# Differential attention over 32 chunks: a loop of four lanes against a pipeline of one chunk a slot, with block-wise scores

## The chip, the cores and the metric

The kernel runs on one core of a Trainium2 chip. The metric is the device time of one execution in microseconds (us). A core has five engines that run side by side and meet at semaphores: TensorE (PE in the profile, its weight loads PEld), VectorE (DVE), ScalarE (ACT), GpSimd (POOL) and SyncE (SP), which here only issues DMAs.

## The reference

Six layers follow one another, each added to its input after a LayerNorm without weights: cross-attention, differential attention, a gated feed-forward layer, an adapter attention, a second attention and a layer of eight experts. Only the second, differential attention, is touched. Its core, cut to what matters:

```python
b, t, e = x.shape                                   # 128 sequences, 32 tokens, 256 features
q = (x @ wq.T).reshape(b, t, NH2, HALF)             # NH2 = 4 half-heads of HALF = 64
k = (x @ wk.T).reshape(b, t, NH2, HALF)
v = (x @ wv.T).reshape(b, t, H, 2 * HALF)           # H = 2 heads of 128
q = _apply_rope(q, cos, sin)
k = _apply_rope(k, cos, sin)
scores = jnp.einsum('bhtd,bhsd->bhts', q, k) / SCALING      # SCALING = 128 ** -0.5
probs = jax.nn.softmax(scores, axis=-1)
lam = lam1 - lam2 + LAMBDA_INIT
probs = probs.reshape(b, H, 2, t, t)
diff = probs[:, :, 0] - lam * probs[:, :, 1]
attn = jnp.einsum('bhts,bhsd->bhtd', diff, v)
attn = attn * jax.lax.rsqrt(jnp.mean(attn * attn, axis=-1, keepdims=True) + EPS)
attn = attn * subln_weight
return attn.transpose(0, 2, 1, 3).reshape(b, t, e) @ wout.T
```

The softmax runs over the 32 tokens of a sequence for each of four half-heads; the probabilities of two half-heads are subtracted with a factor lambda, and the result weighs v. Then comes an RMS norm for each head and the output projection. All is in float32.

## The kernel before, in words

The 128 x 32 tokens are 4096 rows, cut into 32 chunks of 128 rows. So one chunk holds four whole sequences of 32 tokens, one under the other on the partitions. Each of the six layers is a phase of its own with a barrier behind it (`phase`, L2600), so the engines start every phase together.

`differential_attention` (L1294) works on four chunks a turn, one in each of its LANES, in eight turns: seven in a hardware loop (`turns`, L1355) and the last written out behind it. Every engine goes through one step for all four lanes before the next step. The front part of a turn (LayerNorm, transpose, the projections to q, k and v, the rotation) is done for the next turn ("ahead") in the middle of the present one. Tiles exist once for each lane. In PSUM, `TurnRing` (L1206) hands the eight banks round: each step of each lane takes the next bank, and PE waits until what the bank held before has been moved out.

The steps for one chunk are these. VectorE computes bn_stats, bn_aggr and var_eps; GpSimd raises to the power -0.5 (inv_std, L1406); VectorE writes xn (L1590). PE transposes xn (L1432), ScalarE copies it to SBUF (xn_t, L1507), PE projects q and k into one bank of 512 columns (L1445) and v into 256. VectorE multiplies by the cosines (turn_cos, L1598, 512 wide) and, swapped in pairs, by the sines (L1599, L1600, 256 wide each), straight from PSUM, and adds (qk, L1603). PE turns qk over (four transposes); ScalarE copies q_t (L1515) and two half-filled copies of k (k_own, L1518), in which the rows of the other half-head are zero. PE multiplies full 128x128 arrays (L1458): each chunk's 128 queries against all its 128 keys, for four half-heads, so three quarters of the scores are between different sequences. VectorE scales them and adds the mask `same` (-1e30 between sequences, L1611), 128x512 in all, and reduces the negative maximum (L1616). ScalarE takes the exponential with a row sum for each half-head (L1525), each followed by a read of the accumulator. VectorE forms reciprocal, lambda factor, the weighed second half and diff (L1621 to L1626); PE transposes diff, ScalarE copies it, PE multiplies by v (av, L1471). ScalarE squares and sums (L1531), VectorE forms ms (L1632), GpSimd inv_rms (L1413), VectorE attn with both factors (L1637). PE transposes attn, ScalarE copies it, PE applies w_o (L1482), VectorE adds the residual x_res, which was loaded a second time, and SyncE stores y.

Semaphores count by lane and turn; on every engine the order is that of the source.

Of the kernel before, what the change touches and what calls it, by code (L numbers as in the profile page):

```python
# [1205 lines left out]
class TurnRing:  # L1206

    def __init__(self, items, turns, ahead=(), banks=8):
        assert len(items) % banks == 0, len(items)
        self.items, self.banks, self.turns, self.ahead = items, banks, turns, ahead
        self.per_bank = len(items) // banks
        self.of_stage = {s: [n for t, n in items if t == s] for s, _ in items}

    def bank(self, stage, n):  # L1220
        return self.items.index((stage, n)) % self.banks

    def _earlier(self, stage, n, keep):

        at = self.items.index((stage, n))
        return [self.items[k] for k in range(at % self.banks, at, self.banks) if keep(self.items[k][0])]

    def full(self, t, stage, n):

        is_ahead = lambda s: s in self.ahead  # L1230
        if isinstance(t, int) and t == 0 and stage in self.ahead:
            return 1 + len(self._earlier(stage, n, is_ahead))
        first = len([1 for s, k in self.items if s in self.ahead and self.bank(s, k) == self.bank(stage, n)])
        if isinstance(t, int) and t == self.turns - 1 and stage not in self.ahead:
            return first + t * self.per_bank + 1 + len(self._earlier(stage, n, lambda s: not is_ahead(s)))
        body = self.per_bank if stage in self.ahead else 0
        return t * self.per_bank + (first + 1 + len(self._earlier(stage, n, lambda s: True)) - body)

    def out(self, t, stage, n, back=0):

        own = self.of_stage[stage]
        return t * len(own) + (own.index(n) + 1 + len(own) * (1 - back))

    def before(self, t, stage, n):

        is_ahead = lambda s: s in self.ahead
        if isinstance(t, int) and t == 0 and stage in self.ahead:
            held = self._earlier(stage, n, is_ahead)
            return (held[-1][0], self.out(0, *held[-1])) if held else None
        last = isinstance(t, int) and t == self.turns - 1 and stage not in self.ahead  # L1250
        held, wrap = self._earlier(stage, n, (lambda s: not is_ahead(s)) if last else (lambda s: True)), 0
        if not held:
            held, wrap = [(s, k) for s, k in self.items if self.bank(s, k) == self.bank(stage, n)], 1
        s, k = held[-1]
        back = wrap + (stage in self.ahead) - (s in self.ahead)
        return s, self.out(t, s, k, back=back)


# [1383 lines left out]
```

## Time and profile before

| what | us |
|---|---|
| median of three runs | 3857.2 |
| lowest and highest | 3856.8, 3860.03 |
| the profiled execution | 3863.55 |
| its span, first to last instruction | 3861.8 |
| the stage of differential attention, first load to last residual add | 996.71 to 1307.38 |
| one turn of its loop (four chunks) | 35.3 |

Over the span PE is busy 91%, VectorE 66%, ScalarE 52% and GpSimd 39%, at a mean granted clock of TensorE of 0.961 of full speed. These are averages over six phases; for a change to one phase the windows and the timeline of this phase count.

How to read the rows further down. A row of the timeline has the start, the time, the engine, the line, the operation, what is written and read, the shape and the number of instructions, and in brackets the idle time ahead and what ended it; a row for several instructions runs from the first start to the last end. A row of the windows has the stretch, its length, for PE, PEld, DVE, ACT and POOL the busy time with the number of instructions, the granted clock of TensorE, the share of DMA time and GB/s. A row of the groups has after the bar the busy time in all and the mean in ns, then the idle time ahead of the group. A row of the waits has who waited for whom, us in total, how often, and the longest. A row of one line's instructions gives ns as minimum, median and maximum. A float32 product appears as two matmuls, a transpose as one.

### The profile page before, as it was taken

To read this page: it belongs to the slowest core of one execution; us is meant where nothing else is said; L and a number is where in the kernel's file an instruction comes from. 1 tells how busy PE (TensorE), PEld (TensorE's weight loads), DVE (VectorE), ACT (ScalarE), POOL (GpSimd) and SP (SyncE) were. 2 spreads that over 40 slices of the span, in tenths; PEclk is the share of its full clock that TensorE was granted. 3 is DMA by queue.
4 is the path that set the end of the run, shared out by engine and by line. 5 is a ranking of instruction groups with operands and counts; after the bars stand their busy time and mean duration, and the time that the engine had idled before them with its cause. 6 is when DMAs were issued, how large, how long until landed. Compare 5 with 4: busy or idle time off the path is not lost. (4 is left out here: it accounts for less than half of the span.)

```text
span 3861.8 us, 99724 instructions
## 1 busy us (share of the span) xinstructions
PE 3515.5 (91%) x32616; PEld 2584.1 (67%) x32616; DVE 2541.8 (66%) x7637; ACT 1991.8 (52%) x6079; POOL 1509.7 (39%) x3070
## 2 busy tenths in 40 slices
PE   7999999999477797999999999999968869999999
PEld 5777777777355575777777777777746545555555
DVE  4667777777577554888888888888845543344333
ACT  4777777777255444666666666676632211111111
POOL 3566666666111253555555555555520000000000
PEclk9999999999789898999999999999978969999999
DMA  3111111111111123111111111111145650000000
GB/s 82 54 52 50 51 52 52 52 52 40 49 49 49 51 82 93 42 44 43 41 45 42 41 47 40 41 47 40 37 94 128 131 146 18 16 16 16 16 16 16
DMA packets 355951, 200.53 MB, mean 52 GB/s; under 512 B 186126, under 2 KB 350822, under 8 KB 355830
## 3 DMA queue, kind: packets, MB, share of 16 engines
q1 hardware_dynamic: 335669, 189.95, 17.7%
q10 hardware_dynamic: 20160, 8.92, 1.2%
q8 instruction: 82, 1.34, 0.2%
q14 instruction: 40, 0.32, 0.0%
HBM read 154.12 MB, written 40.40 MB: 50 GB/s over the span
## 5 line engine op out<-in xcount | busy, mean ns | idle before, releaser
L1004 ACT ACTIVATE probs_a<-s_ps_a,neg_max_a 128x257 f32<-128x257 f32 x1024 | 474.0, 474 | 368.6 <-DVE neg_max_a L1101 368.6
L1047 POOL TENSOR_SCALAR probs_a<-probs_a,gated_a 128x256 f32<-128x256 f32 x1024 | 497.4, 504 | 310.9 <-DVE gated_a L1109 310.9
L1101 DVE TENSOR_REDUCE neg_max_a<-s_ps_a 128x1 f32<-128x257 f32 x1024 | 361.2, 415 | 0.0
L2458 ACT ACTIVATE gate_e<-bank_e 128x512 f32<-128x512 f32 x128 | 76.4, 597 | 493.4 <-PE bank_e L2431 493.3
L498 POOL TENSOR_SCALAR probs_i<-probs_i,inv_sum_i 128x256 f32<-128x256 f32 x512 | 256.9, 515 | 136.9 <-DVE inv_sum_i L631 135.6
L2390 POOL TENSOR_TENSOR inv_std_e<-var_eps_e,half_e 128x1 f32<-128x1 f32 x32 | 16.5, 541 | 654.0 <-DVE var_eps_e L2489 654.0
L2572 DVE TENSOR_TENSOR hidden_e<-gate_e,bank_e 128x512 f32<-128x512 f32 x128 | 87.4, 688 | 276.1 <-PE bank_e L2431 274.3
L476 ACT ACTIVATE probs_i<-s_ps_i,neg_max_i 128x257 f32<-128x257 f32 x512 | 235.9, 473 | 49.8 <-DVE neg_max_i L692 48.7
L862 PE MATMUL c_ps_a<-ctx_t_a,w_qk_a 128*128 128x256 f32 x1024 | 256.9, 394 | 0.0
L908 PE MATMUL a_ps_a<-w_v_a,ctx_t_a 128*128 128x256 f32 x1024 | 255.3, 392 | 0.0
L369 PE MATMUL a_ps_i<-w_k_i,ctx_t_i 128*128 128x256 f32 x1024 | 253.1, 390 | 1.4 <-issue 0.2
L385 PE MATMUL c_ps_i<-w_v_i,ctx_t_i 128*128 128x256 f32 x1024 | 243.4, 381 | 0.0
L2431 PE MATMUL bank_e<-xn_t_e,w_gate_e 128*128 128x512 f32 x512 | 242.8, 597 | 0.0
L2431 PE MATMUL bank_e<-xn_t_e,w_up_e 128*128 128x512 f32 x512 | 240.6, 592 | 0.0
L692 DVE TENSOR_REDUCE neg_max_i<-s_ps_i 128x1 f32<-128x257 f32 x512 | 182.0, 418 | 80.8 <-PE s_ps_i L427 80.8
L862 PEld LDWEIGHTS c_ps_a<-ctx_t_a,w_qk_a 128*128 128x128 f32 x1024 | 185.2, 191 | 69.3 <-issue 36.0
L908 PEld LDWEIGHTS a_ps_a<-w_v_a,ctx_t_a 128*128 128x128 f32 x1024 | 184.1, 190 | 69.2 <-issue 49.5
L2409 PE MATMUL bank_e<-w_down_e,hidden_e 128*128 128x256 f32 x1024 | 230.2, 379 | 0.0
L2409 PEld LDWEIGHTS bank_e<-w_down_e,hidden_e 128*128 128x128 f32 x1024 | 194.7, 190 | 50.2 <-issue 26.8
L1004 ACT ACTIVATION_READ_ACCUMULATOR probs_a<-s_ps_a,neg_max_a 128x1 f32 x1024 | 207.5, 203 | 0.0
L369 PEld LDWEIGHTS a_ps_i<-w_k_i,ctx_t_i 128*128 128x128 f32 x1024 | 185.3, 191 | 32.7 <-issue 6.3
L869 PE MATMUL s_ps_a<-k_t_a,q_bd_a 32*128 32x289 f32 x2048 | 197.1, 454 | 2.3 <-DVE k_t_a L1188 1.8
(352 smaller groups left out, 8171.5 us busy)
## 6 DMA issues: line engine op xcount, KB each, us to landing
ctx_t_i<-in_ctx_t SPq DMA_DIRECT2D x128, 256.0 KB, 2.7
ctx_t_a<-in_ctx_t SPq DMA_DIRECT2D x128, 256.0 KB, 2.7
mask_a<-in_L_xattn_mask SPq DMA_DIRECT2D x512, 4.0 KB, 1.5
v_bd_a<-v_self_a SPq DMA_DIRECT2D x512, 8.0 KB, 1.8
x_tok_i<-in_x SPq DMA_DIRECT2D x32, 128.0 KB, 2.0
x_res_i<-in_x SPq DMA_DIRECT2D x32, 128.0 KB, 2.5
x_after<-y_tok_i SPq DMA_DIRECT2D x32, 128.0 KB, 1.8
x_tok_d<-x_after SPq DMA_DIRECT2D x32, 128.0 KB, 2.1
```

The source lines that it names most:

```text
L369: last = pe.matmul(a_ps[:, r * D:r * D + D], ctx_t[at.b(2)][:, c, r * P:r * P + P], w_k[:, c, :], start=c == 0, stop=c == 1)
L385: last = pe.matmul(c_ps[:, r * D:r * D + D], ctx_t[at.b(1)][:, c, r * P:r * P + P], w_v[:, c, :], start=c == 0, stop=c == 1)
L476: act.activation(probs[:, i, :], s_ps[i][:, 0:K], ACT.Exp, bias=neg_max[:, i:i + 1], accum_out=row_sum[:, i:i + 1]).then_inc(exp_done, 1)
L498: pool.tensor_scalar(probs[:, i, 0:2 * P], probs[:, i, 0:2 * P], inv_sum[:, i:i + 1], 1.0, ALU.mult, ALU.mult).then_inc(probs_ready, 1)
L862: last = pe.matmul(into[:, f * n:f * n + n], w_qk[:, c, D + f * P:D + f * P + P], ctx[:, c, 0:n], start=c == 0, stop=c == 1)
L869: pe.matmul(s_ps[:, g, 0:N], q_bd[j][rows, f, :, :].rearrange("p h q -> p (h q)"), k_t[j][rows, f, :], start=True, stop=True).then_inc(sco ...
L908: last = pe.matmul(a_ps[:, r * D:r * D + D], ctx_t[at.b(1)][:, c, r * P:r * P + P], w_v[:, c, :], start=c == 0, stop=c == 1)
L1004: act.activation(probs[:, t, :], s_ps[:, g, 0:K], ACT.Exp, bias=neg_max[:, t:t + 1], accum_out=row_sum[:, t:t + 1]).then_inc(exp_done, 1)
L1047: pool.tensor_scalar(probs[:, t, 0:2 * P], probs[:, t, 0:2 * P], gated[:, t:t + 1], 1.0, ALU.mult, ALU.mult).then_inc(probs_ready, 1)
L1101: dve.tensor_reduce(neg_max[:, 4 * f + g:4 * f + g + 1], s_ps[:, g, 0:K], AX.X, ALU.max, negate=True).then_inc(max_ready, 1)
L2409: last = pe.matmul(w[:, t * D:t * D + D], hidden[e % 2][:, k, tok:tok + P], w_down[:, e, k, :], start=k == 0, stop=k == TILES - 1)
L2431: last = pe.matmul(w[:, :], weights[:, e, c, t * P:t * P + P], xn_t[:, c, :], start=c == 0, stop=c == 1)
```

## The change

The function is rewritten; `TurnRing`, the mask and the loop are gone.

- One chunk enters each slot, and the slots, from -3 to 34, are written out one after another without a loop. In slot n the statistics and xn are those of chunk n+3, the transpose of xn is that of n+2, projections and rotation those of n+1, scores to diff those of n, av, squares and inv_rms those of n-1, the scaling, the output projection and the store those of n-2.
- Most tiles exist once. v has three copies, diff_t and y two, x_tok eight; the residual is taken from x_tok, so the second load goes. PSUM has fixed places: a bank each for qk, the transposed qk, av, the transposed attn and y, one shared by v and the transposed xn, and two for the scores.
- Scores are formed for each sequence by itself: 4 sequences x 2 half-heads x 2 heads, products of 64 rows by 32 columns each, side by side in tiles of the array. The result is 128x128 a chunk, 32 keys a half-head, and needs no mask. av is formed in the same manner, 32 rows by 32 columns by 128.
- VectorE reduces the maximum and subtracts it (top, centred); one exponential of 128 columns takes the place of four, with the scale in it and without a row sum, which is a reduction on VectorE.
- diff is turned over by VectorE in blocks of 32x32 (transpose to diff_t) in place of PE and a copy.
- The projection of q and k is copied to SBUF by ScalarE (qk_raw); the two sine products and xn move from VectorE to GpSimd. Scaling attn by inv_rms moves to ScalarE; the weight subln is multiplied into w_o once.
- The loads at the start are split over SyncE's and ScalarE's queue with a semaphore each.

```diff
-    stages = ["qkT", "s0", "s1", "xT", "qk", "dT", "av", "v", "aT", "out"]
-    ring = TurnRing([(s, a) for s in stages for a in range(LANES)], CHUNKS // LANES, ahead=FRONT)
+        SLOTS = range(-3, CHUNKS + 3)
...
+                if live(n + 1):
+                    pairs, sines = (x.rearrange("p (f two) -> p f two", two=2) for x in (qk_raw[:, :], rope[:, 1, :]))
+                    dst = turn_sin[:, :].rearrange("p (f two) -> p f two", two=2)
+                    pool.wait_ge(qk_read, n + 2)
+                    pool.tensor_tensor(dst[:, :, 0], pairs[:, :, 1], sines[:, :, 0], ALU.mult)
+                    pool.tensor_tensor(dst[:, :, 1], pairs[:, :, 0], sines[:, :, 1], ALU.mult).then_inc(sin_ready, 1)
...
+                if live(n - 1):
+                    pool.wait_ge(ms_ready, n)
+                    pool.tensor_tensor(inv_rms[:, :], ms[:, :], half[:, :], ALU.pow).then_inc(rms_ready, 1)
...
+                    pe.wait_ge(qk_t_ready, n + 1)
+                    ge(pe, centred_ready, n)
+                    for c in range(2):
+                        for s in range(4):
+                            own = slice(L * s, L * s + L)
+                            for r in range(2):
+                                rows = slice(HALF * r, HALF * r + HALF)
+                                last = pe.matmul(s_ps[own, r, c * L:c * L + L], qk_t[rows, c, own], qk_t[rows, 2 + c, own], start=True, stop=True)
...
+                if live(n - 2):
+                    act.wait_ge(rms_ready, n - 1)
+                    for h in range(2):
+                        last = act.activation(attn[:, h, :], av_ps[:, h * P:h * P + P], ACT.Copy, scale=inv_rms[:, h:h + 1])
+                    last.then_inc(attn_ready, 1)
+                if live(n + 1):
+                    act.wait_ge(qk_full, n + 2)
+                    ge(act, qk_ready, n + 1)
+                    act.activation(qk_raw[:, :], qk_ps[:, :], ACT.Copy).then_inc(qk_read, 1)
...
+                    dve.wait_ge(exp_done, n + 1)
+                    after(dve.tensor_reduce(row_sum[:, :], probs[:, :, :], AX.X, ALU.add))
+                    after(dve.reciprocal(inv_sum[:, :], row_sum[:, :]))
+                    after(dve.tensor_scalar(inv_sum[:, 2:4], inv_sum[:, 2:4], neg_lam[:, :], None, ALU.mult))
+                    after(dve.tensor_tensor(weighed[:, :, :], probs[:, :, :], inv_sum[:, :].unsqueeze(2).broadcast_to([P, 4, L]), ALU.mult))
+                    after(dve.tensor_tensor(diff[:, :].rearrange("p (c k) -> p c k", c=2), weighed[:, 0:2, :], weighed[:, 2:4, :], ALU.add))
+                    ge(dve, av_full, 4 * (n - 1))
+                    dve.transpose(diff_t[n % 2][:, :], diff[:, :]).then_inc(diff_ready, 1)
+                if live(n - 1):
+                    dve.wait_ge(ss_ready, n)
+                    dve.tensor_scalar(ms[:, :], ss[:, :], 1.0 / P, 1e-5, ALU.mult, ALU.add).then_inc(ms_ready, 1)
```

`after` makes VectorE wait for the instruction before; `ge` waits only where the count is over zero. The function `statistics`, called between the add qk and row_sum, holds bn_stats, bn_aggr and var_eps.

PE's order first. Before, in the last turn (the loop's body has the front steps of the next turn between the scores and the diff transposes), each row is a step of four lanes:

```order
L1432 MATMUL bank_d<-const_d,qk_d 128x128 x16
L1458 MATMUL bank_d<-k_own_d,q_t_d 128x128 x16
L1432 MATMUL bank_d<-const_d,diff_d 128x128 x8
L1471 MATMUL bank_d<-v_d,diff_t_d 128x128 x8
L1432 MATMUL bank_d<-const_d,attn_d 128x128 x8
L1482 MATMUL bank_d<-w_o_d,attn_t_d 128x256 x8
```

Now, one slot from the middle, each row a step of one chunk:

```order
L1348 MATMUL qk_ps_d<-w_qk_d,xn_t_d 128x512 x2
L1354 MATMUL qk_t_ps_d<-ident_d,qk_d 128x128 x4
L1361 MATMUL vx_ps_d<-w_v_d,xn_t_d 128x256 x2
L1371 MATMUL s_ps_d<-qk_t_d 32x32 x16
L1378 MATMUL vx_ps_d<-ident_d,xn_d 128x128 x2
L1384 MATMUL at_ps_d<-ident_d,attn_d 128x128 x2
L1393 MATMUL av_ps_d<-v_d,diff_t_d 32x128 x8
L1402 MATMUL y_ps_d<-w_o_d,attn_t_d 128x256 x2
```

The transposes of diff are gone from PE, the scores stand behind the projection of the next chunk's v, and all eight steps of a slot are of different chunks.

VectorE's order. Before, a part of the last turn, from the last mask to the first lane's diff:

```order
L1611 SCALAR_TENSOR_TENSOR masked_d<-bank_d,same_d 128x256
L1616 TENSOR_REDUCE neg_max_d<-masked_d 128x4
L1621 RECIPROCAL inv_sum_d<-row_sum_d 128x4
L1622 TENSOR_SCALAR inv_sum_d<-inv_sum_d,neg_lam_d 128x2
L1623 TENSOR_TENSOR masked_d<-probs_d,inv_sum_d 128x256
L1626 SCALAR_TENSOR_TENSOR diff_d<-probs_d,inv_sum_d,masked_d 128x128 x2
```

Now, in a middle slot, from the maximum to the block transpose; ahead of it stands turn_cos, behind it ms and y:

```order
L1481 TENSOR_REDUCE top_d<-s_ps_d 128x4
L1482 TENSOR_TENSOR centred_d<-s_ps_d,top_d 128x128
L1488 TENSOR_TENSOR qk_d<-turn_cos_d,turn_sin_d 128x512
L1459 BN_STATS stats_d<-x_tok_d 128x6
L1461 BN_AGGR mean_var_d<-stats_d 128x2
L1462 TENSOR_SCALAR var_eps_d<-mean_var_d 128x1
L1496 TENSOR_REDUCE row_sum_d<-probs_d 128x4
L1497 RECIPROCAL inv_sum_d<-row_sum_d 128x4
L1498 TENSOR_SCALAR inv_sum_d<-inv_sum_d,neg_lam_d 128x2
L1499 TENSOR_TENSOR weighed_d<-probs_d,inv_sum_d 128x128
L1500 TENSOR_TENSOR diff_d<-weighed_d 128x64
L1502 STREAM_TRANSPOSE diff_t_d<-diff_d 128x64
```

Between the maximum and the row sum of one chunk there now stand the add for the next chunk and the statistics of the chunk three on.

GpSimd's order. Before, in the loop's body (two rows of four for each kind shown):

```order
L1406 TENSOR_TENSOR inv_std_d<-var_eps_d,half_d 128x1
L1412 ISA
L1413 TENSOR_TENSOR inv_rms_d<-ms_d,half_d 128x2
L1412 REGISTER_ALU
L1413 TENSOR_TENSOR inv_rms_d<-ms_d,half_d 128x2
```

Now, one slot:

```order
L1326 TENSOR_TENSOR turn_sin_d<-qk_raw_d,rope_d 128x256
L1327 TENSOR_TENSOR turn_sin_d<-qk_raw_d,rope_d 128x256
L1330 TENSOR_TENSOR inv_std_d<-var_eps_d,half_d 128x1
L1333 TENSOR_SCALAR xn_d<-x_tok_d,mean_var_d,inv_std_d 128x256
L1336 TENSOR_TENSOR inv_rms_d<-ms_d,half_d 128x2
```

inv_rms now stands behind the sine products and xn of later chunks.

## Rows read from the trace of the kernel before

**Rows 1.** Timeline at the stage's edges, and from the DMA issues the load of rope (last number: us to landing).

```profile
996.71 1.78 SPq L1370 DMA_DIRECT2D x_tok_d<-x_after  x4
...
1306.96 0.42 DVE L1643 TENSOR_TENSOR y_d<-bank_d,x_res_d 128x256 f32<-128x256 f32 x1 [0.44 <-PE bank_d L1482]
...
rope_d<-in_L_attn_rope SPq DMA_DIRECT2D x1, 512.0 KB, 3.6
```

**Rows 2.** Windows, one turn of the loop.

```profile
1098.30:1133.60 35.30, 27.05 (x136) 19.31 (x135) 26.65 (x80) 18.55 (x76) 4.82 (x8) 0.90 0.14 45
```

**Rows 3.** Waits in the seven turns, 1027.5 to 1275.5.

```profile
PE bank_d L1432 <- DVE xn_d L1590: 43.1, 7, 6.2
...
DVE masked_d L1611 <- PE bank_d L1458: 27.5, 28, 3.0
```

**Rows 4.** ScalarE: a group of 128-wide squares, and two 512-wide copies in the timeline.

```profile
L1531 ACT ACTIVATE squares_d<-bank_d 128x128 f32<-128x128 f32 x64 | 17.1, 273 | 1.9 <-PE bank_d L1471 1.2
...
1325.21 1.08 ACT L1844 ACTIVATE xs_g<-bank_g 128x512 fp32r<-128x512 f32 x2 [0.50 <-PE bank_g L1779]
```

**Rows 5.** PE's timeline in three other stages: transposes, tiles, a projection.

```profile
703.89 0.60 PE L414 MATMUL a_ps_i<-const_i,probs_i 128*128 128x128 f32 x4
...
704.86 0.69 PE L427 MATMUL s_ps_i<-k_n_i,q_bd_i 32*64 32x257 f32 x16
706.17 0.65 PE L437 MATMUL out_ps_i<-probs_t_i,v_i 128*32 128x64 f32 x32 [0.62 <-ACT probs_t_i L472]
...
2685.48 1.88 PE L920 MATMUL b_ps_a<-w_qk_a,xn_t_a 128*128 128x512 f32 x4
...
2905.23 2.48 PE L2112 MATMUL s_ps_r<-by_dim_k_r,by_dim_q_r 32*32 32x64 f32 x128 [0.29 <-DVE attn_r L2296]
```

**Rows 6.** What ended the idle time ahead of L427's weight loads.

```profile
  issue: 22.6, 128
```

**Rows 7.** VectorE: groups by form, and four adds in the timeline.

```profile
L1550 DVE TENSOR_TENSOR lam_in_d<-lam_in_d 128x128 f32<-128x128 f32 x1 | 0.3, 293 | 9.7 <-DMA lam_in_d<-in_L_attn_lambda_k 9.7
...
1125.54 2.48 DVE L1603 TENSOR_TENSOR qk_d<-turn_cos_d,turn_sin_d 128x512 f32<-128x512 f32 x4
...
L1578 DVE BATCH_NORM_STATS2 stats_d<-x_tok_d 128x6 f32<-128x256 f32 x32 | 11.2, 412 | 0.0
...
L1621 DVE RECIPROCAL inv_sum_d<-row_sum_d 128x4 f32<-128x4 f32 x32 | 5.5, 171 | 0.0
...
L1622 DVE TENSOR_SCALAR inv_sum_d<-inv_sum_d,neg_lam_d 128x2 f32<-128x2 f32 x32 | 7.3, 229 | 1.1
...
L1623 DVE TENSOR_TENSOR masked_d<-probs_d,inv_sum_d 128x256 f32<-128x256 f32 x32 | 13.6, 426 | 1.1
...
L685 DVE STREAM_TRANSPOSE p_last_t_i<-p_last_i 128x32 f32<-128x32 f32 x32 | 6.5, 204 | 0.9 <-POOL p_last_i L494 0.9
```

**Rows 8.** Timeline of one turn: from ms over inv_rms to attn.

```profile
1128.18 1.37 POOL L1413 TENSOR_TENSOR inv_rms_d<-ms_d,half_d 128x2 f32<-128x2 f32 x2 [13.90 <-DVE ms_d L1632]
...
1129.00 0.35 DVE L1637 SCALAR_TENSOR_TENSOR attn_d<-bank_d,inv_rms_d,subln_d 128x128 f32<-128x128 f32 x1 [0.70 <-POOL inv_rms_d L1413]
```

**Rows 9.** GpSimd's groups of 256 columns in two other stages.

```profile
L498 POOL TENSOR_SCALAR probs_i<-probs_i,inv_sum_i 128x256 f32<-128x256 f32 x512 | 256.9, 515 | 136.9 <-DVE inv_sum_i L631 135.6
...
L1060 POOL TENSOR_TENSOR self_p_a<-self_e_a,self_inv_a 128x256 f32<-128x256 f32 x128 | 78.6, 614 | 0.0
...
L505 POOL TENSOR_TENSOR v_last_i<-v_last_raw_i,const_i 128x256 f32<-128x256 f32 x32 | 27.3, 853 | 0.0
```

**Rows 10.** One VectorE line of the first stage.

```profile
L674 DVE TENSOR_SCALAR xn_i<-x_tok_i,mean_var_i,inv_std_i x32: 414/931/933, 24.5 to 925.1; 128x256 f32<-128x256 f32 x32
```

**Rows 11.** PE's timeline behind its long idle time, and a window inside it.

```profile
1113.23 2.24 PE L1432 MATMUL bank_d<-const_d,xn_d 128*128 128x128 f32 x8 [6.16 <-DVE xn_d L1590]
...
1110.30:1111.30 1.00, 0.00 (x0) 0.00 (x0) 1.00 (x4) 0.00 (x0) 0.00 (x0) 0.50 0.00 0
```

More of the change, by code:

```diff
@@ L1203, in _ @@
             every_slot(dve, FIRST, TURNS, slot)
[L1206 to L1256, printed above, removed]
 LANES = 4
@@ L1351, in moved @@
-        def moved(i, stage, a, back=0):
-            return out_of[stage], ring.out(i, stage, a, back=back)
-        def turns(eng, body):
-            with eng.Fori(0, TURNS - 1) as i:
-                body(i, i + 1)
-            body(TURNS - 1, None)
-        def free_banks(eng, name):
-            for s in stages:
-                if mover[s] == name:
-                    eng.sem_inc(out_of[s], LANES)
+        x_tok = [sb(f"x_tok{j}", [P, D]) for j in range(X_TILES)]
+        stats, mean_var, var_eps, inv_std = sb("stats", [P, 6]), sb("mean_var", [P, 2]), sb("var_eps", [P, 1]), sb("inv_std", [P, 1])
@@ new lines, in differential_attention @@
+        xn, xn_t = sb("xn", [P, D]), sb("xn_t", [P, 2, P])
+        qk_raw, turn_cos, turn_sin, qk = (sb(n, [P, 2 * D]) for n in ("qk_raw", "turn_cos", "turn_sin", "qk"))
+        qk_t = sb("qk_t", [P, 4, P])
+        v = [sb(f"v{j}", [P, D]) for j in range(3)]
+        top, centred, probs = sb("top", [P, 4]), sb("centred", [P, 4, L]), sb("probs", [P, 4, L])
+        row_sum, inv_sum = sb("row_sum", [P, 4]), sb("inv_sum", [P, 4])
+        weighed, diff = sb("weighed", [P, 4, L]), sb("diff", [P, 2 * L])
@@ L1365, in differential_attention, with live @@
+        at_full, at_ready, y_full, y_ready = sem("at_full"), sem("at_ready"), sem("y_full"), sem("y_ready")
+        step = sem("step")
+        SLOTS = range(-3, CHUNKS + 3)
         block = stack.enter_context(nc.Block())
+        def live(n):
+            return 0 <= n < CHUNKS
         @block.sync
         def _(sp):
[L1369 to L1379 removed]
@@ L1403, in front @@
-            def front(t):
-                for a in range(LANES):
-                    pool.wait_ge(ln_dve, n_of(t, a))
-                    pool.tensor_tensor(inv_std[a][:, :], var_eps[a][:, :], half[:, 0:1], ALU.pow).then_inc(ln_pool, 1)
-            def body(i, ahead):
-                if ahead is not None:
-                    front(ahead)
-                for a in range(LANES):
-                    pool.wait_ge(ms_ready, n_of(i, a))
-                    pool.tensor_tensor(inv_rms[a][:, :], ms[a][:, :], half[:, :], ALU.pow).then_inc(inv_rms_ready, 1)
@@ L1418, in _ @@
         @block.tensor
         def _(pe):
-            pe.wait_ge(loaded, 16 * 12)
-            def item(i, stage, a):
-                held = ring.before(i, stage, a)
-                if held:
-                    pe.wait_ge(out_of[held[0]], held[1])
-                n = ring.bank(stage, a)
-                return bank[n], full[n]
-            def turn_over(i, stage, a, src, count):
-                w, f = item(i, stage, a)
-                for c in range(count):
-                    last = pe.transpose(w[:, c * P:c * P + P], src(c), ident)
-                last.then_inc(f, 1)
```

425 lines of the change are left out of this document (174 added, 251 removed).

## Prediction, made before the changed kernel was run

> **What bounds the kernel now.** I read the windows of the stage first, then its waits, then the timeline. The change touches one stage of six, so only that stage's time can move: it runs from the first load at 996.71 to the last residual add, which ends at 1307.38 (1306.96 + 0.42), 310.7 us of the 3861.8 us span [rows 1]. Inside, a turn of the loop takes 35.3 us for four chunks, 8.8 us a chunk, and no engine fills it: PE 27.1, VectorE 26.7, ScalarE 18.6, GpSimd 4.8 us [rows 2]. The waits say why: the four lanes go through each step together, so the engines take turns. PE waits for xn once a turn, 43.1 us in seven turns, up to 6.2 at once, and VectorE for the scores, 27.5 us [rows 3]. The bound is the hand-over between engines in a turn, not an engine. A pipeline with one chunk a slot attacks just that, and the question is what the slot's own longest loop is.
>
> **The slot, step by step.** In the new order GpSimd's inv_rms for chunk n-1 comes last in slot n; ScalarE's first step of the next slot (scaling attn) waits for it, and everything behind it on ScalarE queues, the copies qk_raw and qk_t among them. The scores wait for qk_t, VectorE's maximum for the scores, and VectorE then runs in order down to ms, for which inv_rms waits. That is a closed loop, and its length is the slot. From mark to mark (the start of the attn scaling):
> - attn, two copies of 128 from PSUM, 0.27 each alone, overlapped to the next start: 0.35; qk_raw, 512 wide, two of which take 1.08, so 0.60 alone and 0.48 to the next start: 0.50; qk_t, whose end counts: 0.60 + 0.04 hop [rows 4]. Together 1.49.
> - scores: 16 products are 32 matmuls here, in tiles of 64 rows x 32 columns. No such tile is in the trace. From below, 32 matmuls of 64 columns in 128x32 tiles take 0.65 and 16 of 257 columns in 32x64 tiles 0.69. From above, 128 strided ones in 32x32 tiles take 2.48, 0.62 for 32; tiles of 64 rows number half as many, and if only half as many run side by side it is 1.24 [rows 5]. The first row is nearest in instructions and width (even a little wider), so I take 0.70 + 0.04.
> - top and centred, each over 128 columns, 0.29 alone: 0.29 + 0.04, and 0.25 to the next start [rows 7]. Together 0.58.
> - the add qk, 512 wide: four in 2.48, the last 0.68, so 0.60 to 0.62 [rows 7].
> - statistics of chunk n+3: 0.41, then two short ones that wait for each other, 0.34 with the gaps (0.16 and less each, by the shortest rows here): 0.75 [rows 7].
> - row_sum 0.29, reciprocal 0.17, the factor 0.23, weighed (128) 0.29, diff (64) 0.22, the block transpose of 64 columns 0.24 (0.20 for 32), and five gaps of 0.035 (1.1 us over 32): 1.64 [rows 7].
> - ms 0.16 and a hop of 0.08; inv_rms, two of which take 1.37, 0.70 and a hop of 0.10 (in the timeline 0.12, from 1128.18 + 0.70 to 1129.00): 1.04 [rows 8].
> The sum is 1.49 + 0.74 + 0.58 + 0.62 + 0.75 + 1.64 + 1.04 = 6.86 us.
>
> **What GpSimd's new work adds.** It takes over the two sine products (256 wide, strided) and xn. A product of that width is 0.61 where nothing hinders it and 0.85 in the first stage [rows 9]. The sines start 1.03 after the mark and the add wants them at 2.81: two at 0.61 end at 2.25, two at 0.85 at 2.73, and if they first wait out turn_cos (0.68) they end at 2.93, which pushes the add by 0.16. Then pow (below the 0.70 of inv_rms) and xn (0.50) on GpSimd lie beside VectorE's weighed and diff. A VectorE instruction can be held for the whole of a GpSimd one: xn_i has a median of 931 ns and a minimum of 414, and the difference is just GpSimd's 515 [rows 9, 10]. So 0 to 0.5 there. I take 0.15 and 0.25, in all 0.4: both meetings happen in every slot, but neither is sure to overlap in full. The slot is 7.25 us, with 6.8 and 7.6 for nothing and everything of this, and 0.5 more if the scores are at their upper end. The Trainium skill (GPSIMD Engine Reference, section Engine selection) says not to put two-input elementwise work on GpSimd, as it is about 2x slower there than on VectorE; this case's rows say 0.61 against 0.43 for VectorE's 256-wide product [rows 7, 9], 1.4x; by twice 0.43 the sines would be 1.72 together, end at 2.75, and still make the add. The rule would be right about the work but not about the loop, because VectorE is in the loop and GpSimd between 1.0 and 2.8 is not.
>
> **The other engines in a slot.** PE: 1.72 + 0.86 + 0.86 for the projections (four instructions of 512 columns in 1.88, so 0.43 each, and half for 256), 0.44 + 0.22 + 0.22 for transposes (four in 0.60, some 0.16 of it latency), 0.60 for scores, 0.45 for av: 5.4 us [rows 5]. It changes its tiling four times a slot. The weight loads of the tiled group at L427 stand idle 22.6 us over 128 groups, 0.18 each; four times that makes 6.1 us [rows 6]. ScalarE 3.6 us, GpSimd 3.1. All are under 7.25, so the other work that goes (masking of 128x128, four exponentials with a read each for one, half-empty k copies) pays only as far as it shortens the loop.
>
> **From slot to stage.** 31 slots separate the marks of slots 1 and 32: 31 x 7.25 = 224.8, less 2.9 as slots 29 to 31 lack statistics and the last the add. Ahead: the loads, where rope (3.6 us to land) [rows 1] holds GpSimd's start to about 1001.5; LayerNorm, a transpose, the projection, rotation, the second transpose and its copy, one after another and partly at the lower clock, 9.5 us to where slot 0's mark would be at 1010 or so; slot 0 with the lambda arithmetic (a 512-wide product and four small ones, 1.6), but without inv_rms, 7 to 9: mark 1 at about 1018.7, 22 us after the first load. Behind mark 32: scaling, av, squares, inv_rms, scaling, transpose, copy, output product 1.03, add 0.42: 6.3. Sum 22 + 221.9 + 6.3 = 250.2 against 310.7: 60.5 us gone. The profiled execution took 3863.55; so 3803; it lies 6.35 over the median of the three runs, which moves alike, to 3797. Outside the stage nothing changes.
>
> **Rivals.**
> - **The loop is longer** (8.1, from 7.75 to 8.8): scores at 1.24, GpSimd holding VectorE for full instructions twice a slot, hops of two waits each. For it: strided operands on GpSimd aren't in the trace, and loops added up leave out small gaps. Against: each piece's row is at hand. 7.25 + 0.85 gives 31 x 0.85 = 26 more: 3823.
> - **The loop is shorter** (6.7): nothing meets on GpSimd, and start-up takes 20: 3797 - 17 - 2 = 3778.
> - **Slower: PE at its lower clock.** In the loop of before PE stands idle for 6.16 us a turn up to 1113.23, and in the microsecond from 1110.30 the granted clock is 0.50, 1.2 GHz [rows 11]. The new slot leaves PE idle in one piece of 1.2 to 2 us, each slot. If the clock goes down there, PE's 5.4 us double to about 10.4 and PE becomes the bound: 31 x 3.15 = 98, 3895 in all. It decides from a slot of 9.2 us on, that is with some 60% of the slots at 1.2 GHz. For it: the idle piece comes every slot. Against: in the loop of before it takes the long idle piece to bring it down, and a PE that has become the bound has no idle left to lower it. No row shows what a piece of 1 to 2 us does.
> - **It does not do what it says:** the straight-line code of 38 slots (the loop of before was one body) or single buffers make slots wait so that 8.85 a chunk stays; 3850 to 3865. Per slot PE needs some 150 instructions in 7 us. Nothing in the trace shows a wait for code of that size.
>
> **Numbers.** Forecast 60%, longer loop 22%, shorter 8%, no change 4%, slower 6%. The likeliest gives 3797. The range takes the longer loop in: a slot of 8.35 gives 31 x 1.1 = 34, so 3832 above; the shorter loop gives 3776 below. A measurement of this kernel can tell about 0.2%, 8 us, from no change; the forecast and both loops lie beyond. Faster 0.90, same 0.04, slower 0.06.
>
> **What would show it.** Right: ScalarE's attn scalings 7.25 us apart (6.9 to 7.7), ahead of each a wait for inv_rms; VectorE waiting for the scores about 1 us a slot and for qk_raw; clock 1.00 from slot 2 on; the last add about 250 us after the first load; VectorE busy some 4.8 us a slot. Wrong step by step: an idle time ahead of the add qk that ends with the sines (GpSimd too slow); weighed or diff over 0.4 us (held port); scores over 1 us; 0.50 in the clock rows inside the stage; PE without idle time at all. A stage at 250 us and a kernel that didn't move would mean another stage gave it back.

## The result and the profile after

The changed kernel takes 3800.3 us (median of four runs, 3797.7 to 3809.5) against 3857.2 us (3856.8 to 3860.0): a ratio of 0.9856 with an interval of 0.984 to 0.9872, 57 us less. The forecast was 3797, with a range of 3776 to 3832, and the measured time lies inside. The profiled execution took 3809.5 us, its span is 3807.7 us, 54.1 less than before. But the stage gave only part of it. Its edges, from the timeline, and the load of rope from the DMA issues:

```profile
998.04 0.36 SPq L1300 DMA_DIRECT2D x_tok_d<-x_after  x1
...
1263.95 0.42 DVE L1509 TENSOR_TENSOR y_d<-y_ps_d,x_tok_d 128x256 f32<-128x256 f32 x1 [3.26 <-PE y_ps_d L1402]
...
1267.59 0.33 SPq L1572 DMA_DIRECT2D ident_g<-in_const  x1
...
rope_d<-in_L_attn_rope ACTq DMA_DIRECT2D x1, 512.0 KB, 6.1
```

From the first load to the last add it is 266.3 us where it was 310.7 [rows 1]: 44.4 us gone, not the 60.5 of the forecast. With the gap to the next stage's first DMA it is 269.6 against 313.9. The remaining 10 us of the two profiles' 54.1 came mostly from a stage that the change does not touch; more on that below. The other 3 us of the 57 come from the choice of execution: the profiled one lies 9.2 us above its median here, 6.4 before.

The slot. Starts of ScalarE's attn are 7.62 or 7.63 us apart in 27 slots of the 31; two windows of a slot each (columns as in [rows 2]):

```profile
1114.74:1122.36 7.62, 7.06 (x77) 4.57 (x75) 4.62 (x15) 3.35 (x13) 4.75 (x5) 1.00 0.12 37
1122.36:1129.98 7.62, 5.96 (x63) 3.89 (x64) 4.62 (x15) 3.46 (x12) 4.75 (x5) 0.78 0.12 34
```

GpSimd is busy 4.75 us, not the 3.1 forecast. The granted clock is 1.00 in one slot and 0.78 in the other, and both last 7.62: TensorE's clock does not set the slot. It is 0.78 in eight of the 27 equal slots. In the last steps, with nothing else in flight, the clock does count. These are the window from the last attn to the end of the last add, and in it the last output product, first in this profile and then in that of e12, which differs only by a table that is loaded and not used:

```profile
1260.00:1264.37 4.37, 2.98 (x7) 1.46 (x6) 0.85 (x2) 1.01 (x3) 0.00 (x0) 0.50 0.09 30
...
1261.84 2.07 PE L1402 MATMUL y_ps_d<-w_o_d,attn_t_d 128*128 128x256 f32 x4 [0.47 <-ACT attn_t_d L1437]
...
1253.59:1256.77 3.18, 1.57 (x6) 0.88 (x6) 0.42 (x1) 1.01 (x3) 0.00 (x0) 1.00 0.12 41
...
1255.18 1.13 PE L1409 MATMUL y_ps_d<-w_o_d,attn_t_d 128*128 128x256 f32 x4 [0.47 <-ACT attn_t_d L1445]
```

At a clock of 0.50 it takes 4.37 us, at 1.00 3.18. The start differs as well: the first attn comes 32.8 us after the first load here and 30.9 in e12, whose stage is 4.7 us shorter with the same slot. So one profile tells the stage to some 5 us, and the slot much better.

The waits of the loop, 1025 to 1235, where [rows 3] had PE waiting for xn and VectorE for the scores:

```profile
ACT attn_d L1417 <- POOL inv_rms_d L1336: 95.9, 27, 3.6
...
DVE turn_cos_d L1478 <- ACT qk_raw_d L1422: 49.0, 27, 2.1
...
DVE qk_d L1488 <- POOL turn_sin_d L1327: 14.8, 27, 0.6
DVE top_d L1481 <- PE s_ps_d L1371: 10.1, 27, 0.4
```

And the chain of one slot, from its timeline:

```profile
1122.36 0.62 ACT L1417 ACTIVATE attn_d<-av_ps_d,inv_rms_d 128x128 f32<-128x128 f32 x2 [3.64 <-POOL inv_rms_d L1336]
1122.87 0.60 ACT L1422 ACTIVATE qk_raw_d<-qk_ps_d 128x512 f32<-128x512 f32 x1
...
1123.50 0.69 DVE L1478 TENSOR_TENSOR turn_cos_d<-qk_raw_d,rope_d 128x512 f32<-128x512 f32 x1 [1.81 <-ACT qk_raw_d L1422]
1123.55 1.35 POOL L1326 TENSOR_TENSOR turn_sin_d<-qk_raw_d,rope_d 128x256 f32<-128x256 f32 x1 [1.22 <-ACT qk_raw_d L1422]
...
1124.01 0.36 PE L1371 MATMUL s_ps_d<-qk_t_d 64*32 64x32 f32 x32 [1.95 <-ACT qk_t_d L1425]
...
1124.86 0.84 POOL L1327 TENSOR_TENSOR turn_sin_d<-qk_raw_d,rope_d 128x256 f32<-128x256 f32 x1
1124.89 0.29 DVE L1482 TENSOR_TENSOR centred_d<-s_ps_d,top_d 128x128 f32<-128x128 f32 x1
...
1125.73 0.69 DVE L1488 TENSOR_TENSOR qk_d<-turn_cos_d,turn_sin_d 128x512 f32<-128x512 f32 x1 [0.55 <-POOL turn_sin_d L1327]
...
1127.04 0.20 ACT L1444 ACTIVATION_READ_ACCUMULATOR squares_d<-av_ps_d 128x1 f32 x1
...
1127.89 1.37 POOL L1333 TENSOR_SCALAR xn_d<-x_tok_d,mean_var_d,inv_std_d 128x256 f32<-128x256 f32 x1
...
1128.20 0.46 DVE L1500 TENSOR_TENSOR diff_d<-weighed_d 128x64 f32<-128x64 f32 x1
...
1128.86 0.13 DVE L1505 TENSOR_SCALAR ms_d<-ss_d 128x2 f32<-128x2 f32 x1
...
1129.23 0.72 POOL L1336 TENSOR_TENSOR inv_rms_d<-ms_d,half_d 128x2 f32<-128x2 f32 x1
```

The loop is the one forecast, except for one stretch. The scores' way was open at 1125.18, when centred ended; the add qk began at 1125.73, when the second sine product had ended. So the loop runs over the sines: 1.19 us from attn to the first sine product, 2.18 for both and the hop, 0.61 for the add to its next start, 0.74 statistics, 1.78 from row_sum to ms, 0.37 to inv_rms, 0.75 to the next attn: 7.62. All of it is in a fixed order on each engine, so a step waits for what stands before it even where its input is there: the squares were done at 1127.24, while inv_rms began at 1129.23.

### The profile page after: what moved, and what is told of

Read it like the earlier page. It is cut to its first block and busy times, and to the rows that moved or that the text cites. A ratio compares the mean times of both kernels' runs of the same rounds, so it can differ in the third digit from the quotient of the medians.

```text
span 3807.7 us, 100837 instructions
## 1 busy us (share of the span) xinstructions
PE 3493.5 (92%) x33704; PEld 2547.5 (67%) x33704; DVE 2475.0 (65%) x7474; ACT 1951.9 (51%) x5855; POOL 1621.9 (43%) x3166
## 5 line engine op out<-in xcount | busy, mean ns | idle before, releaser
L363 PEld LDWEIGHTS a_ps_i<-w_k_i,ctx_t_i 128*128 128x128 f32 x1024 | 185.6, 191 | 32.8 <-issue 6.4
```

The lines of the kernel that those rows point to most:

```text
L363: last = pe.matmul(a_ps[:, r * D:r * D + D], ctx_t[at.b(2)][:, c, r * P:r * P + P], w_k[:, c, :], start=c == 0, stop=c == 1)
```

## Experiments

Theory A: the slot is the closed loop over inv_rms, lengthened by GpSimd. Theory B: PE with its tilings is the bound. Theory C: VectorE's work is. "Stage" below is first DMA to first DMA of the next stage in the profile, "rest" the span less the stage, "slot" the usual spacing of attn's starts in the middle of the stage (before: a turn over four). Stage, slot and rest are of one profiled execution each. The variants e1 to e8, e11 and e12 are of the changed kernel, e9 and e10 of the one before. e11 leaves out the swap of pairs and the mean, and is a single run. Ratios are against the kernel before on the same chip.

| kernel | median us | ratio (interval) | stage | slot | rest |
|---|---|---|---|---|---|
| before | 3857.2 | | 313.9 | 8.83 | 3547.9 |
| after | 3800.3 | 0.9856 (0.984-0.9872) | 269.6 | 7.62 | 3538.1 |
| e1, ms early | 3762.4 | 0.9751 (0.9733-0.977) | 224.9 | 6.24 | 3536.7 |
| e2, xn on VectorE | 3792.7 | 0.9827 (0.9807-0.9846) | 255.9 | 7.21 | 3535.6 |
| e3, output product twice | 3800.7 | 0.9854 (0.9836-0.9872) | 266.6 | 7.63 | 3528.6 |
| e4, cosines from PSUM | 3791.2 | 0.9822 (0.9802-0.9842) | 254.6 | 7.12 | 3539.0 |
| e5, ms first | 3748.5 | 0.9706 (0.969-0.9723) | 213.2 | 5.87 | 3535.6 |
| e6, e1 and e4 | 3764.7 | 0.9754 (0.9738-0.977) | 232.0 | 6.42 | 3530.7 |
| e7, scores twice | 3799.9 | 0.9846 (0.9829-0.9862) | 269.5 | 7.63 | 3529.4 |
| e8, sines on VectorE | 3786.0 | 0.981 (0.9794-0.9827) | 253.7 | 7.20 | 3533.0 |
| e9, before again | 3856.6 | 1.0001 (0.9992-1.0011) | 315.9 | | 3541.6 |
| e10, before written out | 3852.1 | 0.9992 (0.9982-1.0001) | 315.6 | | 3532.0 |
| e11, plain GpSimd | 3776.0, one run | | 244.9 | 6.83 | 3529.3 |
| e12, mask table kept | 3794.9 | 0.9846 (0.9829-0.9862) | 264.9 | 7.62 | 3527.8 |

**e1: ms and inv_rms earlier.** In both engines' order only:

```diff
                     after(dve.reciprocal(inv_sum[:, :], row_sum[:, :]))
+                    if live(n - 1):
+                        dve.wait_ge(ss_ready, n)
+                        dve.tensor_scalar(ms[:, :], ss[:, :], 1.0 / P, 1e-5, ALU.mult, ALU.add).then_inc(ms_ready, 1)
...
                     pool.tensor_tensor(inv_std[:, :], var_eps[:, :], half[:, 0:1], ALU.pow).then_inc(ln_pool, 1)
+                if live(n - 1):
+                    pool.wait_ge(ms_ready, n)
+                    pool.tensor_tensor(inv_rms[:, :], ms[:, :], half[:, :], ALU.pow).then_inc(rms_ready, 1)
+                if live(n + 3):
                     pool.wait_ge(ln_pool, n + 4)
```

> The same work in another order: ms of chunk n-1 stands behind the reciprocal on VectorE and no longer behind the block transpose, and inv_rms stands ahead of xn on GpSimd. Theory A (the slot is the closed loop that inv_rms ends): in the changed kernel's middle slot the squares were done at 1127.24 but inv_rms began only at 1129.23; here it can begin at about 1127.9, so 1.3 us less a slot, a slot of 6.1 to 6.4 until PE's own 5.4 to 6.1 us is next: 31 x 1.2 = 37, some 3762 us. Theory B (PE with its tiling switches is the bound): nothing moves, 3795 to 3803. Theory C (VectorE's sum of work and short gaps is the bound, about 7 us a slot): 10 us or less.

Measured: 3762.4 us, slot 6.24. The same instructions, and 1.38 us a slot less. Timeline:

```profile
1125.88 0.17 DVE L1501 TENSOR_SCALAR ms_d<-ss_d 128x2 f32<-128x2 f32 x1
...
1126.13 0.70 POOL L1333 TENSOR_TENSOR inv_rms_d<-ms_d,half_d 128x2 f32<-128x2 f32 x1
...
1126.82 1.23 POOL L1337 TENSOR_SCALAR xn_d<-x_tok_d,mean_var_d,inv_std_d 128x256 f32<-128x256 f32 x1
...
1126.86 0.63 ACT L1418 ACTIVATE attn_d<-av_ps_d,inv_rms_d 128x128 f32<-128x128 f32 x2 [2.25 <-POOL inv_rms_d L1333]
```

The mark (the start of attn) follows inv_rms at once, as before the edit. The 1.38 us are the time from row_sum to ms, 0.52 instead of 1.78, and from ms to inv_rms, 0.25 instead of 0.37. That shows theory A and rules out B and C: on both engines the instructions are the same.

**e2: xn back on VectorE**, behind y:

```diff
-                    pool.tensor_scalar(xn[:, :], x_tok[(n + 3) % X_TILES][:, :], mean_var[:, 0:1], inv_std[:, :], ALU.subtract, ALU.mult).then_inc(xn_ready, 1)
...
+                    dve.tensor_scalar(xn[:, :], x_tok[(n + 3) % X_TILES][:, :], mean_var[:, 0:1], inv_std[:, :], ALU.subtract, ALU.mult).then_inc(xn_ready, 1)
```

> One part undone: xn goes back to VectorE, at the end of its slot, where it waits for qk_raw anyway. Theory A: inv_rms no longer stands behind xn (0.2 to 0.3 us) and diff is not stretched (0.45 to 0.22), VectorE's 0.41 more lies in its idle time: 0.4 to 0.5 us less a slot, 3785 us. Theory B: nothing. Theory C: 0.41 more a slot, 3813 us. If GpSimd's instruction holds VectorE's, diff will be 0.22 to 0.25 here; if diff is slow by itself it stays at 0.45.

```profile
1126.97 0.22 DVE L1497 TENSOR_TENSOR diff_d<-weighed_d 128x64 f32<-128x64 f32 x1
...
1127.40 0.13 DVE L1502 TENSOR_SCALAR ms_d<-ss_d 128x2 f32<-128x2 f32 x1
...
1127.61 0.70 POOL L1333 TENSOR_TENSOR inv_rms_d<-ms_d,half_d 128x2 f32<-128x2 f32 x1 [1.03 <-DVE ms_d L1502]
```

The slot is 0.41 shorter, as expected: diff takes 0.22 without xn beside it (0.46 with it), and from ms to inv_rms it is 0.21 instead of 0.37. VectorE's additional 0.41 cost nothing. The stage fell by 14 us, but the kernel's time by 8, less than the 15 expected, and the intervals of this and the changed kernel just touch; it is the slot that shows it.

**e3: the output product twice.**

```diff
-                    for c in range(2):
+                    for c in range(4):
```

(with `c % 2` in the operands)

> The output product is formed twice (four more matmuls of 256 columns a slot, 0.8 to 0.9 us of PE), at the end of PE's slot. Theory A: PE has 1.5 to 2 us of idle time there, so nothing or up to 3 us in all: 3798 to 3803. Theory B (PE is the bound): 0.85 x 31 = 26 us more, 3826.

```profile
1130.81 1.99 PE L1402 MATMUL y_ps_d<-w_o_d,attn_t_d 128*128 128x256 f32 x8
```

Eight matmuls take 1.99, four 1.13 at full clock (e12's row above): 0.86 us more of PE in each slot, and the slot is 7.63. B is out a second time.

**e7: the scores twice**, the 32 matmuls repeated:

```diff
-                    for c in range(2):
+                    for t in range(4):
+                        c = t % 2
...
```

> The 32 matmuls of the scores are run twice a slot. They lie in the loop, unlike the output product of e3. One set takes 0.36 us in the trace. Theory A: the slot grows by 0.33 to 0.36, 31 x 0.34 = 10.5 us, 3811, though only 0.34 us of PE are added where 0.86 off the loop cost nothing. Theory B: nothing to 3 us.

```profile
1130.91 0.76 PE L1372 MATMUL s_ps_d<-qk_t_d 64*32 64x32 f32 x64 [1.61 <-ACT qk_t_d L1426]
...
1131.74 0.29 DVE L1482 TENSOR_REDUCE top_d<-s_ps_d 128x4 f32<-128x128 f32 x1 [0.64 <-PE s_ps_d L1372]
...
1132.64 0.69 DVE L1489 TENSOR_TENSOR qk_d<-turn_cos_d,turn_sin_d 128x512 f32<-128x512 f32 x1 [0.29 <-POOL turn_sin_d L1327]
```

A miss: 3799.9 and a slot of 7.63, no change. top comes 0.27 later (2.48 after the mark, not 2.21), and the wait ahead of the add shrinks from 0.55 to 0.29. So the scores are not on the path; the sines are, with half a microsecond to spare beside them. I had counted the scores into the loop although the trace already showed the add waiting for the sines.

**e4: turn_cos from PSUM**, ahead of the copy:

```diff
-                    dve.wait_ge(qk_read, n + 2)
-                    dve.tensor_tensor(turn_cos[:, :], qk_raw[:, :], rope[:, 0, :], ALU.mult).then_inc(cos_ready, 1)
+                    dve.wait_ge(qk_full, n + 2)
+                    dve.tensor_tensor(turn_cos[:, :], qk_ps[:, :], rope[:, 0, :], ALU.mult).then_inc(cos_ready, 1)
...
+                    act.wait_ge(cos_ready, n + 2)
                     act.activation(qk_raw[:, :], qk_ps[:, :], ACT.Copy).then_inc(qk_read, 1)
```

> turn_cos reads the projection straight from PSUM, ahead of ScalarE's copy qk_raw, which waits for it; VectorE is idle there. So no VectorE product over two SBUF operands runs beside the first sine product. If VectorE's product holds GpSimd's (0.69 of the 1.35 us), the first sine product falls to 0.66 to 0.85, the add qk starts 0.5 us earlier, behind centred, and the slot is 0.5 us shorter: 3785 us. If the strides make it slow, it stays at 1.3 us and the time stays at 3800, or rises a few us as qk_raw comes later.

```profile
1143.60 0.68 DVE L1479 TENSOR_TENSOR turn_cos_d<-qk_ps_d,rope_d 128x512 f32<-128x512 f32 x1
...
1144.35 0.62 ACT L1417 ACTIVATE attn_d<-av_ps_d,inv_rms_d 128x128 f32<-128x128 f32 x2 [3.13 <-POOL inv_rms_d L1336]
...
1145.54 0.84 POOL L1326 TENSOR_TENSOR turn_sin_d<-qk_raw_d,rope_d 128x256 f32<-128x256 f32 x1 [1.22 <-ACT qk_raw_d L1423]
...
1146.33 0.85 POOL L1327 TENSOR_TENSOR turn_sin_d<-qk_raw_d,rope_d 128x256 f32<-128x256 f32 x1
...
1146.88 0.29 DVE L1483 TENSOR_TENSOR centred_d<-s_ps_d,top_d 128x128 f32<-128x128 f32 x1
...
1147.22 0.69 DVE L1489 TENSOR_TENSOR qk_d<-turn_cos_d,turn_sin_d 128x512 f32<-128x512 f32 x1
```

The first sine product fell from 1.35 to 0.84: the turn_cos beside it had added 0.51. The add now begins 2.87 after the mark instead of 3.37, and the slot fell by 0.50. The stage fell by 15 us and the kernel's time by 9, of 15 expected; its interval just touches that of the changed kernel. The edit does two things at once: turn_cos reads PSUM, and it is over before the sines begin. No run separates them. But in the changed kernel the second sine product runs beside top and centred, which read PSUM, and takes 0.84, so that VectorE's work alone does not hold GpSimd. The Trainium skill (SBUF — State Buffer, section "SBUF: two separate sides") describes a port pair shared by the two engines, taken as a lock by a VectorE instruction with two SBUF inputs or by GpSimd. The first sine product agrees nearly: turn_cos had 0.64 us to go when it began, and it took 0.51 longer. The same page of the Trainium skill also says that the loser waits for the whole instruction; diff does not agree: it grew by 0.24 us beside an xn of 1.37 and ended 0.60 before it.

**e8: the sines on VectorE**, behind turn_cos:

```diff
-                    pool.tensor_tensor(dst[:, :, 0], pairs[:, :, 1], sines[:, :, 0], ALU.mult)
-                    pool.tensor_tensor(dst[:, :, 1], pairs[:, :, 0], sines[:, :, 1], ALU.mult).then_inc(sin_ready, 1)
...
+                    dve.tensor_tensor(dst[:, :, 0], pairs[:, :, 1], sines[:, :, 0], ALU.mult)
+                    dve.tensor_tensor(dst[:, :, 1], pairs[:, :, 0], sines[:, :, 1], ALU.mult).then_inc(sin_ready, 1)
```

> One part undone: the two sine products are back on VectorE, behind turn_cos, reading qk_raw. By the trace: turn_cos to 1124.19, two products at 0.43 to 1125.05, top and centred to 1125.68, add from 1125.72, where it began at 1125.73 with GpSimd. So by this the slot changes by 0 to 0.25 us, and pow and xn are not earlier, 3798 to 3806: the work that was moved away was hidden, but only as far as it then held up the add. If the products over strided SBUF operands are slower than 0.43 on VectorE (0.6), 0.3 to 0.4 more a slot, 3812.

```profile
1128.71 0.42 DVE L1475 TENSOR_TENSOR turn_sin_d<-qk_raw_d,rope_d 128x256 f32<-128x256 f32 x1
...
1129.05 0.42 DVE L1476 TENSOR_TENSOR turn_sin_d<-qk_raw_d,rope_d 128x256 f32<-128x256 f32 x1
...
1129.91 0.68 DVE L1486 TENSOR_TENSOR qk_d<-turn_cos_d,turn_sin_d 128x512 f32<-128x512 f32 x1
```

A miss to the good side: 3786.0, slot 7.20. I had counted 0.43 for each sine product on VectorE; they take 0.42, but the next instruction starts 0.34 after each, and the add begins 2.95 us after the mark (1126.96) instead of 3.37. Moving the sines to GpSimd cost 0.42 us a slot. Its interval (0.9794 to 0.9827) lies wholly below that of the changed kernel.

**e11: what makes GpSimd slow.** e4 with plain operands:

```diff
-                    pool.tensor_tensor(dst[:, :, 0], pairs[:, :, 1], sines[:, :, 0], ALU.mult)
+                    pool.tensor_tensor(turn_sin[:, 0:D], qk_raw[:, 0:D], rope[:, 1, 0:D], ALU.mult)
...
-                    pool.tensor_scalar(xn[:, :], x_tok[(n + 3) % X_TILES][:, :], mean_var[:, 0:1], inv_std[:, :], ALU.subtract, ALU.mult).then_inc(xn_ready, 1)
+                    pool.tensor_scalar(xn[:, :], x_tok[(n + 3) % X_TILES][:, :], inv_std[:, :], None, ALU.mult).then_inc(xn_ready, 1)
```

> As e4 (turn_cos from PSUM, so that nothing holds GpSimd), but the sine products read and write plain 256-column halves instead of every second column, and xn is one operation, a product with inv_std, instead of a subtraction and a product; the pair swap and the mean are left out, only the durations count. If the stride makes 0.84 us out of 0.61, the sine products take 0.61 here; if GpSimd takes that long for any product of 256 columns in this stage, 0.84. If the second operation makes xn 1.37, it takes 0.5 to 0.75 here; if it is contention with VectorE's products, 1.2 or more.

The groups, 1025 to 1200:

```profile
L1333 POOL TENSOR_SCALAR xn_d<-x_tok_d,inv_std_d 128x256 f32<-128x256 f32 x26 | 27.9, 1074 | 2.6
...
L1327 POOL TENSOR_TENSOR turn_sin_d<-qk_raw_d,rope_d 128x256 f32<-128x256 f32 x25 | 18.2, 728 | 0.0
```

Between the two guesses: the stride makes 0.12 of the 0.84 us, the second operation (or the second scalar that it reads) 0.30 of the 1.37. Another 0.14 goes with what runs beside it: in e1, where xn stands behind weighed and diff and not beside them, it takes 1.23. Why a product with a scalar takes 1.07 here and 0.515 in the first stage [rows 9] stays open.

**e5 and e6: how far it goes.** e5 places ms right behind the add qk, ahead of the statistics, and inv_rms right behind the sines, ahead of pow:

```diff
+                if live(n - 1):
+                    dve.wait_ge(ss_ready, n)
+                    dve.tensor_scalar(ms[:, :], ss[:, :], 1.0 / P, 1e-5, ALU.mult, ALU.add).then_inc(ms_ready, 1)
                 if live(n + 3):
                     statistics(n + 3)
...
```

e6 has the edits of e1 and e4 together.

> The step of e1 taken further: ms stands right behind the add qk on VectorE (the squares were done at 1124.61 in e1, the add at 1124.70), and inv_rms right behind the two sine products on GpSimd, ahead of pow and xn. Theory A says that the loop by inv_rms is then no longer the longest. What is next: PE, busy 27.2 of 30 us in e1 at full clock, that is 5.65 us of a slot of 6.24. Expected 5.7 to 5.95 a slot: 31 x 0.4 = 12 us less than e1, 3750. If GpSimd (4.7 us of work a slot, xn now last) becomes late for the sines instead, the slot stays at 6.1 to 6.3: 3758 to 3765.

> The edits of e1 and of e4 together. If gains add up: 37.4 + 0.35 x 31 = 11 more than e1, 3751. Against it: in e1 qk_raw starts at 1127.38, and turn_cos could start at 1127.35 at the earliest, behind y, so that it pushes qk_raw to 1128.05, and two sine products at 0.84 end at 1130.35 against 1130.21 in e1. I expect this: the gain of e4 lay in VectorE's idle time before qk_raw, which e1 has used up, so 3760 to 3766.

One slot of e5, the window, and what PE waits for from 1025 to 1180:

```profile
1120.51:1126.39 5.88, 5.60 (x70) 3.63 (x69) 4.62 (x16) 3.58 (x13) 4.72 (x6) 1.00 0.14 45
...
PE vx_ps_d L1378 <- ACT v_d L1428: 7.3, 26, 0.3
```

e5 takes 3748.5 us, 52 less than the changed kernel and the best here. PE is busy 5.60 of 5.88 us at full clock, and the 0.28 between are its wait for ScalarE's copy of v, so PE is very likely the next bound; no run tests it. e6, 3764.7, is no better than e1: its slot is 6.42, not 6.24. ScalarE now waits for turn_cos, which stands behind y:

```profile
ACT qk_raw_d L1424 <- DVE turn_cos_d L1480: 16.6, 26, 2.0
```

The gain of e4 lay in VectorE's idle time ahead of qk_raw, which e1 had already used.

**e9, e10, e12: the stage that was not touched.** Reshaped attention, from its first load to the next stage's, took 322.0 us before and 311.8 after. The window before and, from its waits, PE's "issue" (idle time in which it waited for nothing that the profile shows) at the line of the product with v_pos; then the same for the changed kernel, and for e10:

```profile
2837.80:3159.80 322.00, 237.60 (x6592) 168.63 (x6592) 155.76 (x338) 71.95 (x96) 9.09 (x9) 0.82 0.58 124
...
PE s_ps_r L2126 <- issue: 37.1, 21, 3.6
```

```profile
2793.80:3105.60 311.80, 235.51 (x6592) 167.00 (x6592) 156.23 (x338) 72.20 (x96) 9.09 (x9) 0.82 0.57 128
...
PE s_ps_r L1987 <- issue: 26.1, 18, 3.9
```

```profile
2836.77:3145.92 309.15, 233.93 (x6592) 166.01 (x6592) 155.84 (x338) 72.57 (x96) 9.09 (x9) 0.82 0.58 129
...
PE s_ps_r L2126 <- issue: 29.6, 17, 3.4
```

The same instructions; at this line PE's issue shrank by 11 us, and PE's busy time by 2; other waits grew by some 3. e9 is the kernel before, unchanged; e10 differs from it in this:

```diff
-            with eng.Fori(0, TURNS - 1) as i:
+            for i in range(TURNS - 1):
```

e12 is the changed kernel with the mask table among its inputs:

```diff
-"L0_attn_rope0": rope_table(), "L0_attn_subln"
+"L0_attn_rope0": rope_table(), "L0_attn_same": same_sequence(), "L0_attn_subln"
...
+            act.dma_start(same[:, :], io["same"]).then_inc(w_o_in, 16)
...
```

> The kernel before, unchanged, to see how long its other five stages take in a second profile. In the first one they take 3547.9 us (span 3861.8 less 313.9 from the stage's first DMA to the next stage's), in the nine profiles of the changed kernel and its variants 3528.6 to 3539.0; most of it lies in reshaped attention, 322.0 us against 301.8 to 313.0. If the first profile was an outlier, the rest takes 3530 to 3539 here and the stage carries the whole difference of the medians. If it is something lasting, 3545 to 3550, with reshaped attention at 318 or more.

> The kernel before with the stage's seven turns written out one after another in place of the hardware loop; the same instructions are executed, but the code that follows lies elsewhere, as in the changed kernel, and more code is fetched. If where the code lies makes reshaped attention longer, it falls here to 302 to 313 us and the kernel by some 10 us, to 3847. If not, 3857, and the stage itself within 3 us of 313.9: written-out code by itself costs nothing.

> The changed kernel, but the mask table (64 KB) stays among the inputs, where it stood, and is loaded once and not used, so that all inputs and buffers behind it lie in memory as in the kernel before. The stages outside differential attention take 3528.6 to 3539.0 us in the changed kernel and its variants, 3547.9 and 3541.6 in two profiles of the kernel before, 3532.0 with its loop written out. If the place of the data in memory makes the difference, they take 3541 or more here and the kernel 3808 to 3812. If not, 3529 to 3539, and 3797 to 3803.

The difference seems to last: the rest takes 3547.9 and 3541.6 in the two profiles of before, 3533 on average (3527.8 to 3539.0) in eleven of the new code, which differ by up to 11 us among themselves. The place of the data is not it: e12 stays at 3527.8. The place or the amount of code before it may be: e10, the same work written out, has a rest of 3532.0 and reshaped attention at 309.1 (315.9 in e9), with 29.6 us of issue at that line. But its median is only 4.5 us below e9's, over ten runs each, and its interval reaches 1.0001. So some 10 us come from the rest; that they come from where the code lies, or how much there is of it, is possible and not shown. Also, e10's stage is 315.6: written-out code alone gains nothing there.

## Why the prediction was right and where it was not

- **The bound.** Right: hand-over between engines, no single engine. e1 and e3 show it. The loop over inv_rms is the slot.
- **The scores.** The way from the mark to the end of centred was put at 2.81 and is 2.82, but by errors that cancel: the 32 matmuls take 0.36, not 0.70, while they begin 0.16 later and top starts 0.20 behind their end, not 0.04. That is luck. It didn't matter, since the path runs over the sines.
- **The sines: the step that failed most.** They were put at 0.61 to 0.85 each and to end 2.25 to 2.93 after the mark; they end at 3.34 (1.35 and 0.84). The forecast had the case "they first wait out turn_cos", but then went on at 0.61 instead of 0.84. They also began at 1.19, not 1.03. 0.15 us was set aside; the add waits 0.55.
- **xn.** Put at 0.50, measured 1.37, so it also keeps inv_rms waiting, for which the sum had nothing. The hold on diff was put at 0.25 and is 0.24. In all GpSimd costs 0.55 + 0.24 + 0.16 = 0.95 against 0.40. Smaller terms gave 0.19 back: 0.10 from row_sum to ms without the hold (1.54, not 1.64; the prediction's own rows add up to 1.62), 0.08 from ms over inv_rms to the mark without xn (0.96, not 1.04), 0.01 in the rest. So 6.86 + 0.95 - 0.19 = 7.62 against 7.25.
- **The rule of the Trainium skill against the change** (GPSIMD Engine Reference, section Engine selection: two-input elementwise work is about 2x slower on GpSimd). I set it aside because "VectorE is in the loop and GpSimd between 1.0 and 2.8 is not". This case's trace agrees: 0.84 against 0.42 in e8, just 2x. By that alone the sines would have ended at 1.19 + 1.68 = 2.87, close to centred; it is the 0.51 beside turn_cos that made them late. e8 shows that VectorE was the better place for them in this kernel.
- **The other engines.** PE 5.67 us a slot in e1, inside 5.4 to 6.1; ScalarE 3.4 (3.6). GpSimd 4.75 against 3.1, by the same mis-sized rows.
- **From slot to stage.** 266.3 against 250.2: 31 x 0.37 = 11.5 from the slot, 3.5 at the start (the first attn 32.8 after the first load, not 22 + 7.25 = 29.3; rope took 6.1 us to land, not 3.6), and the remaining 1 is what is left for the end, where the clock of 0.50 made the last steps longer.
- **"Outside the stage nothing changes."** Wrong by some 10 us, and this made up for most of the 16 that the stage lacked; another 3 went because the profiled execution lay 9.2 us above the median, not 6.35. So 3797 came out 3 us from the median with a stage 16 us too short: right in sign and mechanism, lucky in the last digits.
- **PE at its lower clock** came, against "clock 1.00 from slot 2 on", but only for a part of some slots: 0.78 in eight of 27. The prediction had no row for idle pieces of 1 to 2 us; here they do go with a lower clock at times, and in e3, where PE has 0.86 us more to do in each slot, the clock is 1.00 from the second slot on. It cost nothing in the loop, where a slot at 0.78 is as long as one at 1.00, since PE has slack.
- **Its own signs.** Of those for a wrong step three came: an idle time ahead of the add that ends with the sines (0.55), diff over 0.4 (0.46), and the lower clock inside the stage.
- **The longer loop** was put at 8.1, in part for causes that are there (GpSimd holding VectorE, strided operands), in part for one that is not (scores at 1.24); the slot of 7.62 lies between it and the forecast.

## What to carry to other kernels

In a pipeline with one item a slot, write down the closed loop and look for the instruction in it whose input has long been there: here moving ms and inv_rms ahead (e5) gave 52 us, about as much as the whole rewrite. Work moved to GpSimd is free only if it ends before its reader wants it. Here a product took 0.84 us there against 0.42 on VectorE, and 1.35 beside a VectorE product over two SBUF operands; add it up with such prices, and look at what stands behind it in GpSimd's queue. Compare the untouched stages of the two traces before crediting a change with the difference.
